# VectorE turns x of chunk 1 and B of chunk 0 to tokens in the paired groups of a Mamba-2 layer kernel

## The reference

```
proj = hidden @ in_proj_w.T            # gate (4096), x (4096), B (8 x 128), C (8 x 128), dt (64)
xBC  = silu(causal_conv4(proj[x, B, C]))
dt_p = softplus(dt + dt_bias);  dA = exp(dt_p * -exp(A_log))
state = state * dA + (dt_p * x) (outer) B        # per head: 64 heads of 64, 8 groups of heads share B and C
y     = C . state + D * x
y     = y * rsqrt(mean(y*y) per group + eps) * norm_weight * silu(gate)
out   = y @ out_proj_w.T
```

## Time and profile before

| what | value |
|---|---|
| median of the runs | 3176.2 us |
| the profiled execution: its own time / its span | 3177.18 / 3175.3 us |
| granted TensorE clock | 1.000 of full speed, in the whole span |
| PE busy | 3157.5 us, 99% |
| PE weight loads busy | 2598.2 us, 82% |
| DVE busy | 2469.2 us, 78% |
| ACT busy | 1550.1 us, 49% |
| POOL busy | 857.4 us, 27% |

### The profile page before, as it was taken

One profiled execution on the slowest core, in us unless ns is written; L12 is line 12 of the kernel. 1 busy time (PEld: TensorE's weight loads), 2 busy tenths in 40 slices (PEclk: granted clock), 3 DMA queues, 4 the chain that ended last, 5 costly groups with the idle time before them and its releaser, 6 DMA issues.

```text
span 3175.3 us, 55177 instructions
## 1 busy us (share of the span) xinstructions
PE 3157.5 (99%) x17933; PEld 2598.2 (82%) x17933; DVE 2469.2 (78%) x4773; ACT 1550.1 (49%) x3816; POOL 857.4 (27%) x917
## 2 busy tenths in 40 slices
PE   8999999999999999999999999999999999999999
PEld 7788888887888888888788888888878888888887
DVE  7977777786588888888658888888855888888883
ACT  5666656663364444454235544445423545444441
POOL 4444434343032222222102222222210222222220
PEclk9999999999999999999999999999999999999999
DMA  8777777776665555556476555556557655555554
GB/s 288 273 269 263 265 276 261 277 258 255 238 208 183 189 187 192 187 187 209 160 234 201 185 188 189 196 181 194 196 170 237 193 192 186 192 189 197 183 189 159
DMA packets 185666, 672.63 MB, mean 212 GB/s; under 512 B 21056, under 2 KB 22208, under 8 KB 185408
## 3 DMA queue, kind: packets, MB, share of 16 engines
q1 hardware_dynamic: 161280, 584.91, 54.6%
q10 hardware_dynamic: 24128, 84.42, 7.9%
HBM read 532.41 MB, written 136.84 MB: 211 GB/s over the span
## 4 chain that ended last, share of the span: by engine, by line
PE 95%; DVE 3%; ACT 1%; DMA 1%; issue 0%; SPq 0%; ACTq 0%; DVEq 0%
PE dense L1040 27%; PE dense L1042 27%; PE dense L1041 27%; PE pY L1140 3%; PE pD L1170 2%; PE pD L1140 1%; DVE conv_us L1452 1%; PE pCB L1116 1%; PE pU L1040 1%; PE dense L1077 1%; PE pS L1041 1%; PE pS L1040 1%; PE pU L1042 1%; PE pS L1042 1%; PE pU L1041 1%; PE pX L1110 1%
## 5 line engine op out<-in xcount | busy, mean ns | idle before, releaser
L1040 PE MATMUL dense<-xn_hi,w_hl 128*128 128x512 f32 (+1 forms) x2888 | 1143.2, 396 | 1.4 <-POOL w_hl L437 0.8
L1042 PE MATMUL dense<-xn_hi,w_hl 128*128 128x512 f32 (+1 forms) x2888 | 1125.1, 390 | 0.0
L1041 PE MATMUL dense<-xn_lo,w_hl 128*128 128x512 f32 (+1 forms) x2888 | 1123.6, 389 | 0.0
L1042 PEld LDWEIGHTS dense<-xn_hi,w_hl 128*128 128x128 f32 (+1 forms) x2888 | 540.1, 187 | 115.7
L1040 PEld LDWEIGHTS dense<-xn_hi,w_hl 128*128 128x128 f32 (+1 forms) x2888 | 540.7, 187 | 114.4 <-issue 3.0
L1041 PEld LDWEIGHTS dense<-xn_lo,w_hl 128*128 128x128 f32 (+1 forms) x2888 | 540.9, 187 | 110.9 <-issue 1.9
L1452 DVE SCALAR_TENSOR_TENSOR conv_us<-conv_in,const_g,conv_us 128x512 f32<-128x512 f32 x576 | 466.2, 810 | 138.8 <-ACT conv_us L686 123.2
L1040 PE MATMUL dense<-z_hi,w_hl 128*128 128x512 f32 x1024 | 406.0, 397 | 1.9 <-DVE acc L1606 1.4
L1042 PE MATMUL dense<-z_hi,w_hl 128*128 128x512 f32 x1024 | 399.3, 390 | 0.0
L1041 PE MATMUL dense<-z_lo,w_hl 128*128 128x512 f32 x1024 | 398.7, 389 | 0.0
L493 POOL TENSOR_TENSOR C_lo<-BC,C_hi 128x128 fp32r<-128x128 f32 x120 | 73.5, 613 | 1191.0 <-ACT S_hi L724 1190.3
(11 more groups left out here) (205 smaller groups left out, 4610.1 us busy)
## 6 DMA issues: line engine op xcount, KB each, us to landing
w_hl<-w_split SPq DMA_DIRECT2D x732, 512.0 KB, 3.5
w_split<-w_hl SPq DMA_DIRECT2D x244, 512.0 KB, 3.6
cum_b<-cum_scratch ACTq DMA_DIRECT2D x128, 512.0 KB, 5.0
w_raw<-w_slots_dram SPq DMA_DIRECT2D x122, 512.0 KB, 5.2
acc<-x_tr_dram ACTq DMA_DIRECT2D x16, 512.0 KB, 6.0
out_tr_dram<-acc ACTq DMA_DIRECT2D x16, 512.0 KB, 4.7
BC<-x_tok_dram SPq DMA_DIRECT2D x6, 512.0 KB, 5.0
conv_us<-x_tok_dram SPq DMA_DIRECT2D x6, 512.0 KB, 5.8
```

Of the source, the lines that this page charges most:

```text
L1040: nc.tensor.matmul(out, lhs[0], rhs[0], start=start, stop=False)
L1041: nc.tensor.matmul(out, lhs[0], rhs[1], start=False, stop=False)
L1042: return nc.tensor.matmul(out, lhs[1], rhs[0], start=False, stop=stop)
```

## The change

In the paired groups, VectorE turns x for chunk 1 as well, and B for all four chunks. PE's transposes of both go away. The sweep over B moves out of its place among the first additions, to the end of the group before: in two parts of eight instructions in a paired group, in one of 16 at the end of group 0. In the freed place stand the 16 instructions for x of chunk 1: four ahead of `y_state`, four ahead of addition 0, eight ahead of addition 1. Addition 2 (the first of output unit 1) moves from behind all of chunk 1's products on DVE to a place between `chunk_1_x` and `chunk_1_rest`. The number of PSUM banks for the dense units stays two.

```diff
-        B_tm = sb("B_tm", [128, NC - 1, N])
+        B_tm = sb("B_tm", [128, NC, N])
...
-        BY_DVE = (0, 2, 3)
+        BY_DVE = (0, 1, 2, 3)
...
-                    if two and c > 0:
+                    if two:
                         act.wait_ge(bt_done, bt_n(q, g))
-                    nc.scalar.activation(B_hi[:], B_tm[:, c - 1, :] if two and c > 0 else pCB[:, 0:N], ACT.Copy).then_inc(ck_evac, 1)
+                    nc.scalar.activation(B_hi[:], B_tm[:, c, :] if two else pCB[:, 0:N], ACT.Copy).then_inc(ck_evac, 1)
...
-                    chunk_1(g, 0, p, 0 in BY_DVE, False)
+                    chunk_1(g, 0, p, True, True)
...
-                    chunk_1(g, 1, p, 1 in BY_DVE, True)
+                    chunk_1(g, 1, p, True, True)
...
-                        dve.wait_ge(ck_evac, chunk(q, g, 0) + 1)
-                        dve.wait_ge(bl_done, chunk(q, g, 0) + 1)
+                        dve.wait_ge(ck_evac, chunk(q, g, 0))
+                        dve.wait_ge(bl_done, chunk(q, g, 0))
...
+                        if not first_block:
+                            B_rows(g + 1, 1 - p, 0, 4)
                         prep(g + 1)
...
+                    x_rows(g, 1, p, 0, 1)
                     y_state(g, 0, True)
                     y_skip(g, 0, True)
                     gate_tile(g, 3, False)
                     state(g, 0)
                     dve.wait_ge(acc_loaded, (q + 1) * 64)
-                    B_rows(g, p, 0, 1)
+                    x_rows(g, 1, p, 1, 2)
                     out_adds(g, 0, halves=(0,))
-                    B_rows(g, p, 1, 3)
+                    x_rows(g, 1, p, 2, 4)
                     out_adds(g, 0, halves=(1,))
-                    B_rows(g, p, 3, 4)
                     if not last:
                         consts_next(g, p)
-                    chunk_1(g, 1, True)
+                    chunk_1_x(g, 1, True)
                     out_adds(g, 1, halves=(0,))
+                    chunk_1_rest(g, 1, True)
                     x_rows(g, 2, p, 0, 1)
...
+                    if not last:
+                        B_rows(g + 1, 1 - p, 0, 2)
                     gated(g, 2)
                     save_state(g)
                     gated_lo(g, 2)
...
                         silu(g, 5, 1 - p)
+                        B_rows(g + 1, 1 - p, 2, 4)
                         prep(g + 1)
```

More of the change, by code:

```diff
@@ L1307, in paired_group @@
                     chunk_2y(g, 1, True)
-                    chunk_1(g, 2, p, 2 in BY_DVE, True)
+                    chunk_1(g, 2, p, True, True)
                     out_units(g, 3)
@@ L1315, in paired_group @@
                     chunk_3(g, 1, two=True)
-                    chunk_1(g, 3, p, 3 in BY_DVE, True)
+                    chunk_1(g, 3, p, True, True)
                     x_units(2)
@@ L1489, in B_rows @@
                         dve.wait_ge(post, post_n(q, g, XT))
-                        dve.wait_ge(ck_evac, chunk(q, g, 0) + 1)
-                        dve.wait_ge(bl_done, chunk(q, g, 0) + 1)
+                        dve.wait_ge(ck_evac, chunk(q, g, 0))
+                        dve.wait_ge(bl_done, chunk(q, g, 0))
                     for f in range(first, end):
                         for k in range(4):
-                            src = BT[p][32 * f:32 * f + 32, :].rearrange("n (c t) -> n c t", c=NC)[:, 1:NC, 32 * k:32 * k + 32]
+                            src = BT[p][32 * f:32 * f + 32, :].rearrange("n (c t) -> n c t", c=NC)[:, :, 32 * k:32 * k + 32]
                             ins = nc.vector.transpose(B_tm[32 * k:32 * k + 32, :, 32 * f:32 * f + 32], src)
@@ L1518, in chunk_1_rest @@
                     nc.vector.tensor_tensor(CBm, pCB[:, N:N + Q], causal[:], ALU.mult).then_inc(cbm_done, 1)
-                    nc.vector.tensor_tensor(B_lo[:], B_tm[:, c - 1, :] if two and c > 0 else pCB[:, 0:N], B_hi[:].bitcast(F32), ALU.subtract)\
+                    nc.vector.tensor_tensor(B_lo[:], B_tm[:, c, :] if two else pCB[:, 0:N], B_hi[:].bitcast(F32), ALU.subtract)\
                         .then_inc(bl_done, 1)
```

## The result

The changed kernel takes 3219.4 us (median of 4 runs, 3218.4 to 3220.4), the kernel before 3176.6 us in the same session: a ratio of 1.0136, with a 95% interval of 1.0122 to 1.0149. It is slower by 42.8 us, 1.4%; the forecast was slower by 33. The span of the profiled execution went from 3175.3 to 3218.0 us.

The account below looks back on a forecast made before the run. PE, busy 99% of the span, was taken to bound the kernel. Lags of PE behind DVE, 18 x 1.41 + 3 x 2.54 = 33.0 us, on 3176.2 gave 3209 us, range 3174 to 3233.

Parts of the forecast that it names:

- its nearest rival: Chunk 1's products: as forecast, but POOL doesn't hold up `xD`; addition 1 decides, 22.4 us slower, 3199 us; chance 0.24.
- Step 1: End of the group: transposes of B, partly filling DVE's 1.58 us wait, make `tok_g` and `x_tm` 3.46 us late.
- Step 2: Products of chunk 0: `dtx` and `wx` no longer wait for POOL, 1.63 us come back, DVE late by 1.83.
- The rival in which this wait stays: Products of chunk 0: POOL starts later than estimated, all lags grow by 1.63 us, 3243 us; chance 0.08.
- Step 3: Output half 0: ACT ends the third gate unit just in time for PE; no wait, no slack left.
- the sign that step 2's gain did not come: Before output half 0: PE idle time ended by ACT or `z_lo` would show the 1.63 us were not won back.
- Steps 4 and 5: Additions 0 and 1: late by 2.2 and 2.46 us, PE 0.2 and 0.82 us behind its old time.
- Step 6: Addition 2, moved ahead of three operations, is in time; addition 3 is late by 1.33, PE 0.28 us behind.
- Step 7: Chunk 1's `xD` waits for POOL, 1.13 us more; addition 3 is late by 2.46, PE 1.41 us behind.
- The largest counts, not the sum: PE's waits within a paired group: only the largest lag lengthens the group, 1.4 us; lesser ones are covered.
- The sum: All 21 paired groups: 18 at 1.41 us and 3 (group 7) at 2.54, 33.0 us in all.
- The chance of a faster kernel: Additions: DVE keeps up, addition 1 at most 1.09 us late; full saving gives 3164.6 us; chance 0.13.

## Why the prediction was right

The direction and the mechanism held: PE's instructions went away, DVE's chain in a group became longer than PE's slack, and the additions hold PE up. The size was 10 us short: 3219.4 us lies at the top end, 3219, of what the forecast and its nearest rival spanned with their errors, and well inside the stated range only because that reached to 3233. By its steps:

- *Step 1, end of the group.* `x_tm` is 3.64 us late, 3.46 was said. The difference is mostly small gaps before and behind each sweep, which the working left out.
- *Step 2, the wait for POOL vanishes.* Shown: `dtx` and `wx` take 0.69 each. POOL's decay starts at 1217.36, 0.25 later by its own row once 4.26 is taken off, where 0.2 was estimated, and it is done before `dtx` (POOL's row in the changed kernel is below). Chunk 0's products were then 2.0 us late (the end of `wx`; said: 1.83). The rival in which this wait stays (3243 us) falls.
- *Step 3, half 0.* "Just in time" was a wait of 0.29 us for ACT, and 0.15 behind. The kernel with B alone shows it by itself. The prediction had named idle time here, ended by ACT, as the sign that step 2's gain did not come. The sign was drawn too sharp: the gain came, and 0.2 us of lateness more than said are enough for the wait.
- *Steps 4 and 5.* Addition 0 2.42 late (said 2.2), addition 1 2.71 (2.46). PE behind by 0.49 and 1.12 (0.2 and 0.82). Besides the carried lateness, the slack is 0.05 us smaller than I took it, since PE's load starts that much behind an addition's end (1235.03 + 0.69 to 1235.77 is 0.05 us).
- *Step 6.* Addition 2 0.60 late, in time.
- *Step 7, `xD` meets POOL.* Shown by its 1.77 us, and by the two kernels that move it away: 0.68, and 7 to 10 us less in the total. The term was 1.13 and measured 1.09. Addition 3 is 2.82 late (2.46) and PE 1.82 behind (1.41). The rival without it was priced at step 5's 0.82 for a middle group. That lag itself measured 1.12, and the kernel that comes nearest to the rival shows 1.2, as addition 2 comes to decide there.
- *"The largest counts, not the sum", "not handed on".* Both true in a middle group: behind half 5 PE's lag stays at 1.72 to 1.79 in blocks 1 and 2 (1.86 to 1.91 in block 3, one 2.21), and the next group starts from there, not higher.
- *The sum.* A middle group was sized at 1.41 and measured 1.8 as a rule; the 18 groups other than group 7 sum to 32.8 us where 25.4 was said. Group 7 was sized at 2.54 and measured 3.94, 3.94 and 2.91: 3.2 us more in all, some 2 us of it the half-speed stretches told of below. The two errors, 7.4 and 3.2, less the 0.8 won elsewhere, make up the 10 us between 3209 and 3219. The first error is one of small things nearly all in one direction: 0.25 us more lateness at addition 1 and 0.36 at addition 3 than worked out, and a slack that is 0.05 smaller.
- *The chance of a faster kernel* needed addition 1 to be late by at most 1.09. It was 2.71, and no second gain like that of step 2 came.

The row of POOL that step 2 rests on:

```profile
1217.36 1.05 POOL L497 TENSOR_TENSOR S_cur<-S_cur,tok_g 128x512 f32<-128x512 f32 x1
```

**The rule on the shared port.** "Who interferes with whom" (the Trainium skill, SBUF — State Buffer) says that a VectorE instruction with two SBUF inputs contends with a GpSimd one that reads SBUF for a port that only one can hold. The trace agrees: with `xD` beside POOL and without, an operation of DVE on two SBUF inputs that comes behind POOL's waits to its end, one that reads PSUM (addition 2, 0.67 us beside POOL) doesn't, and transposes with one SBUF input don't either (1.24 for four). It is so the other way round too: POOL's `C_lo` takes 0.46 us beside transposes (group 4) and 1.39 in group 6, where it begins beside `xD` and ends 0.33 us behind DVE's `z_lo`.

## To carry to other kernels

When an engine is "80% busy", read its timeline between two things that the bounding engine waits for, and write down for each wait how late it may be: here 1.64 and 1.05 us in a stretch that was filled but for one gap of 1.03, and 5 us more had no place there, while a group's end took 5 us for nothing, once of B and once of x (no run has both there). Work that feeds a later stage is put inside a wait, behind the step that the partner needs: the waits of 1.58 us for PE and 1.74 for ACT absorbed it there. An engine that comes late to a wait gets the time back where the partner doesn't need it (1.03 us before `y_state`); where the partner waits for it in turn (1.55 us), the wait stays and the lateness moves along. And put operations that read two SBUF inputs ahead of the moment when the other engine on the port gets its data, with those that read PSUM behind it.

## What was unexpected in the hardware

**The clock after a wait.** In group 7 of blocks 1 and 2, behind a wait of 2.42 us, PE runs for 3.41 us with the granted clock at half, 1.2 instead of 2.4 GHz. Windows of the changed kernel, in order: duration, busy time of PE, PEld, DVE, ACT and POOL, granted clock, DMA share, GB/s:

```profile
1505.00:1508.40 3.40, 1.06 (x6) 0.75 (x4) 3.31 (x8) 2.30 (x8) 1.13 (x2) 1.00 0.70 230
1509.70:1513.00 3.30, 3.30 (x9) 2.53 (x9) 3.13 (x8) 0.85 (x3) 0.38 (x1) 0.50 0.58 216
1514.00:1520.00 6.00, 6.00 (x30) 4.95 (x29) 5.84 (x14) 0.60 (x1) 0.95 (x1) 1.00 0.78 257
```

Its timeline of PE, the start of half 2 and two matmuls in the slow stretch, 0.43 us apart where they are otherwise 0.23:

```profile
1508.49 0.50 PE L1040 MATMUL dense<-z_hi,w_hl 128*128 128x512 f32 x1 [2.42 <-DVE acc L1606]
...
1509.83 0.63 PE L1042 MATMUL dense<-z_hi,w_hl 128*128 128x512 f32 x1
1510.26 0.63 PE L1040 MATMUL dense<-z_hi,w_hl 128*128 128x512 f32 x1
```

It costs about 1 us, the difference between group 7 there (3.94) and in block 3 (2.91), where the same wait (2.44 us) leaves the clock at 1.00. With addition 2 put back it is the other way round: no drop behind the wait of 2.41 in block 1,

```profile
1506.60 0.50 PE L1040 MATMUL dense<-z_hi,w_hl 128*128 128x512 f32 x1 [2.41 <-DVE acc L1606]
```

but one in block 3, and group 7 is 3.87 us longer there and 2.86 and 2.90 in the others. The kernel with x alone moved had 21 waits of 2.19 to 2.52 us and 14 such stretches, each beginning within 1.3 us of the end of one of them. Its groups 1 to 6 in blocks 1 and 2 are 3.67 to 3.75 us longer without one and 3.66 to 3.91 with one: the wait for addition 3 came behind the stretch and covered most of it. The kernels whose longest wait before a half was 1.5 us (the changed kernel with the router moved, in both places) had none. What decides between two equal waits stays open. It also means that a wait of PE of 2.2 to 2.5 us may cost up to one more, which the working did not have.

**Small operations beside POOL.** The router's products of 128x4 and 128x32 have hardly any work, and yet took 1.0 to 1.4 us beside POOL. In that stretch POOL's operations end at 1458.17, 1459.32 and 1460.63, and the products of L1729, L1731 and L1735 end at 1458.19, 1459.37 and 1460.78: each waited for one of POOL's, so short operations in a row pay once for each of them.
